# The order of loads, fills and sums set by kind of unit, large or small, in a shifted depthwise convolution

## The reference

```
def _L0_conv_ref(x, offset):          # 48 offsets, a multiple of 16 px plus a small draw
    off_px = offset * 64.0
    off_int = round(off_px)           # whole shift; sub = the rest
    shifted = x moved by off_int (dx, dy) per channel, zero outside
    kern = exp(-(kx*kx + ky*ky) / (2*0.5*0.5)); kern /= kern.sum()   # 3 x 3, from sub
    return depthwise_conv(shifted, kern, padding='SAME')

def _gn(v, G=32, eps=1e-5):
    g = v.reshape(B, G, C // G, H, W)
    return (g - mean(g)) / sqrt(var(g) + eps)

x = x + _L0_conv_ref(_gn(x), offset)
```

## Time and profile before

| what | value |
|---|---|
| median of 3 runs | 1114.45 us (1113.13 to 1116.01) |
| the profiled execution's own time | 1114.61 us |
| its span | 1112.8 us |
| mean granted TensorE clock | 0.872 |
| VectorE busy | 835.0 us, 75% |
| TensorE busy | 833.4 us, 75% |
| ScalarE busy | 661.0 us, 59% |
| moved by DMA | 403.07 MB, 362 GB/s over the span |

### The profile page before, as it was taken

How to read it: one execution, slowest core, us unless ns; L and a number is a source line. 1 busy time by engine, 2 the same in 40 slices (tenths; PEclk the granted TensorE clock), 3 DMA queues, 4 the chain that set the end, 5 groups by cost and what they waited for, 6 DMA issues and landing times. The chain is left out here.

```text
span 1112.8 us, 9630 instructions
## 1 busy us (share of the span) xinstructions
PE 833.4 (75%) x2176; PEld 399.4 (36%) x2176; DVE 835.0 (75%) x565; ACT 661.0 (59%) x547; POOL 170.7 (15%) x204
## 2 busy tenths in 40 slices
PE   6976986678688698759848887888888686888710
PEld 2432433234343244324324443343444343443310
DVE  8187696976948768696784968787887858659685
ACT  0564546565477574766556666556566474666771
POOL 3103131012110303201211110111112101102010
PEclk9988898989799898888969899898999889788955
DMA  9737979898899797989799999999999897997936
GB/s 373 309 148 274 430 291 400 345 382 373 343 403 412 287 429 320 410 328 398 319 347 429 396 402 428 398 429 398 430 398 433 336 426 305 399 431 306 373 160 292
DMA packets 27818, 403.07 MB, mean 362 GB/s; under 512 B 3216, under 2 KB 3216, under 8 KB 3216
## 3 DMA queue, kind: packets, MB, share of 16 engines
q1 hardware_dynamic: 27792, 402.71, 88.6%
HBM read 201.38 MB, written 201.33 MB: 362 GB/s over the span
## 5 line engine op out<-in xcount | busy, mean ns | idle before, releaser
L243 PE MATMUL sum_ps<-xs,bands 128*128 128x512 f32 x1024 | 505.4, 651 | 23.9 <-DMA xs<-x_dram 23.9
L346 ACT ACTIVATE unused<-xs,small 128x4096 bf16 (+1 forms) x96 | 356.1, 3709 | 20.7 <-ACT small L339 7.7
L499 DVE SCALAR_TENSOR_TENSOR smooth<-frame,xs 128x1700 f32 (+5 forms) x96 | 163.6, 1704 | 220.7 <-ACT frame L320 141.6
L243 PEld LDWEIGHTS sum_ps<-xs,bands 128*128 128x128 f32 x1024 | 209.1, 210 | 270.9 <-issue 267.5
L243 PE MATMUL sum_ps<-xs,halves 128*128 128x512 f32 x512 | 246.3, 637 | 74.2 <-DMA xs<-x_dram 74.2
L313 ACT ACTIVATE frame<-xs,small (+1 forms) x96 | 223.4, 2327 | 130.7 <-DVE smooth L502 128.2
L209 POOL TENSOR_TENSOR small<-small 128x3 f32<-128x3 f32 x32 | 60.9, 1902 | 900.3 <-ACT small L352 900.3
L506 DVE SCALAR_TENSOR_TENSOR xs<-smooth,small,xs 128x1700 f32 (+5 forms) x96 | 163.6, 1704 | 36.5 <-POOL small L221 34.0
L243 PEld LDWEIGHTS sum_ps<-xs,halves 128*128 128x128 f32 x512 | 102.3, 204 | 216.8 <-issue 122.8
L502 DVE SCALAR_TENSOR_TENSOR smooth<-frame,xs,smooth 128x1700 f32<-128x1700 f32 (+5 forms) x96 | 163.5, 1704 | 3.4
L509 DVE SCALAR_TENSOR_TENSOR xs<-smooth,small,xs 128x594 f32 (+9 forms) x96 | 159.8, 1665 | 3.4
(11 more groups left out here) (81 smaller groups left out, 279.0 us busy)
## 6 DMA issues: line engine op xcount, KB each, us to landing
xs<-x_dram SPq DMA_DIRECT2D x96, 2048.0 KB, 14.7
out_dram<-xs SPq DMA_DIRECT2D x96, 2048.0 KB, 11.8
smooth<-offset_dram SPq DMA_DIRECT2D x1, 48.0 KB, 4.0
```

The costliest lines, as they stand in the source:

```text
L243: last = nc.tensor.matmul(sum_ps[:, :], (FIRST, SAME, SECOND)[i], slot_px(n, c * BANK, (c + 1) * BANK), start=(i == 0 and c == 0), stop=(i ...
L346: nc.scalar.activation(unused[:, :], xs[:, bass.ds(n % SLOTS * PIX, PIX)], ACT.Square, bias=neg_mean[:, i:i + 1], accum_out=squares[:, i:i ...
L499: V.scalar_tensor_tensor(sm, frame_window(-1), side_w[:, bass.ds(n, 1), 0], frame_window(0), ALU.mult, ALU.add).wait_op(frame_ready, done_ ...
```

## The change

Three orders are changed, and nothing else.

- SyncE: of the six loads of a pair, those of tiles 6k+10 and 6k+14 move up by one store, ahead of the stores of tiles 6k+2 and 6k+6. The other four stay.
- TensorE: for u even, one tile of sums of u+1 comes before the variances of u and two behind it; for u odd it stays two and one.
- ScalarE: the units with u even use `large_unit`, where variances comes first and sum_means, means and the first square of u+1 come behind the fill of tile 1. The units with u odd use `small_unit`, which is the order before, but with the second square ahead of the fill of tile 2. The loop runs over pairs of units.

```diff
             for n in range(TILES):
                 store(n)
-                if 1 <= n <= TILES - SLOTS:
-                    load(n - 1 + SLOTS)
+                for i in AGAIN[n % len(AGAIN)]:
+                    m = n - n % len(AGAIN) + i + SLOTS
+                    if m < TILES:
+                        load(m)
...
             for u in range(UNITS):
-
+                ahead = 1 if u % 2 == 0 else 2
                 if u + 1 < UNITS:
-                    sums(u + 1, range(UT - 1))
+                    sums(u + 1, range(ahead))
                 variances(u)
                 if u + 1 < UNITS:
-                    sums(u + 1, range(UT - 1, UT))
+                    sums(u + 1, range(ahead, UT))
                     means(u + 1)
...
-            def unit_of(u, ahead=True):
-
+            def large_unit(u):
+
+                variances(u)
+                fill_frame(u, 0)
+                next_fill(u, 0)
+                fill_frame(u, 1)
+                next_fill(u, 1)
+                sum_means(u + 1)
+                means(u + 1)
+                square(u + 1, 0)
+                fill_frame(u, 2)
+                next_fill(u, 2)
+                means_to_fill(u + 1)
+                square(u + 1, 1)
+                square(u + 1, 2)
+
+            def small_unit(u, ahead=True):
                 fill_frame(u, 0)
                 next_fill(u, 0)
                 variances(u)
...
                 if ahead:
                     means(u + 1)
                     square(u + 1, 0)
+                    square(u + 1, 1)
                 fill_frame(u, 2)
                 if ahead:
                     next_fill(u, 2)
                     means_to_fill(u + 1)
-                    square(u + 1, 1)
                     square(u + 1, 2)
...
-            unit_of(0)
+            large_unit(0)
             act.addr_align(256, max_nops=0)
-            with act.Fori(1, UNITS - 1) as u:
-                unit_of(u)
-            unit_of(UNITS - 1, ahead=False)
+            with act.Fori(0, UNITS // 2 - 1) as pair:
+                small_unit(act.snap(2 * pair + 1))
+                large_unit(act.snap(2 * pair + 2))
+            small_unit(UNITS - 1, ahead=False)
```

More of the change, by code:

```diff
@@ L180, in _ @@
                 load(n)
+            AGAIN = [(), (0, 1), (), (2,), (3,), (4, 5)]
             for n in range(TILES):
                 store(n)
-                if 1 <= n <= TILES - SLOTS:
-                    load(n - 1 + SLOTS)
+                for i in AGAIN[n % len(AGAIN)]:
+                    m = n - n % len(AGAIN) + i + SLOTS
+                    if m < TILES:
+                        load(m)
             for s in range(SLOTS):
```

## The result

| kernel | median us (lowest to highest) | ratio to before, 95% interval |
|---|---|---|
| before | 1113.89 (1113.13 to 1116.01) | |
| after | 1124.53 (1123.15 to 1126.43) | 1.0094 [1.0073, 1.0114] |

The change costs 10.6 us, 0.94%. The forecast was 6.4 us slower, 1121.0; the sign and the range hold, and the forecast's own narrow range (1117.5 to 1127) holds it too.

A forecast was written before the change was run, and what follows sets the result against it. A chain through engines waiting in a ring sets the time, transfers close behind. Terms -2.8 (pairs 0, 1), -0.9 (4, 5), +1.8 (3200 pairs), +3.6 (8 to 11), +4.7 (14, 15) give +6.4: 1121.0 us, range 1105 to 1130.

The forecast's parts named there:

- The branch of two tiles: Two tiles of sums behind a large unit's variances take 16.6 us, making the third tile's fill late in some pairs.
- T: Time when TensorE has done a large unit's variances; the next was forecast at T+61.4, against 60.5 a pair before.
- The warm third tile: Sums of the next large unit's third tile, after a 1 to 2 us TensorE pause: 7.1 us in place of 9.53.
- pairs 8 to 11: Pairs with windows like pair 10, where the two-tile branch binds: +0.9 us each, +3.6 in all.
- pairs 14 and 15: First tiles of 900 and 1700 elements, where VectorE needs less time and the branch bites more: +4.7 us together.
- The six pairs of 3200 elements: Pairs 2, 3, 6, 7, 12, 13: VectorE's 18 us first tile covers the branch; net +1.8 us in all.
- Variances ahead of the fill: Large unit's first fill comes 1.7 us later, VectorE's 1.52 us wait for GpSimd goes; net +0.2 to +0.3 a pair.
- the fill ahead of sum_means: Fill of tile 6k+1 no longer waits for TensorE's sums; gain kept in pairs 0 and 1, -0.8 and -2.0 us.
- the other reading in the forecast: GpSimd's small instructions could stick beside VectorE's previous tile through shared SBUF interfaces, leaving up to 1.5 us of the wait.
- Pairs 0 and 1: VectorE leads by more than the branch needs, so they keep the gain of the earlier second fill: -2.8 us.
- The two loads: Loads issued up to 13 us earlier; no load ends last in the chain as read, so taken as 0.

The follow-up runs named there:

- e1: The changed kernel with TensorE's part undone, two tiles of sums ahead of the variances for every unit: 1116.71 us, 1.0021 of before.
- e5: The changed kernel itself, measured once more: 1124.67 us, 1.0094 of before.
- e3: The changed kernel with SyncE's part undone, store and load in turn: 1121.82 us, 1.0059 of before.
- e4: ScalarE's part of the change alone, with TensorE's and SyncE's orders as before: 1136.50 us, 1.0194 of before.
- e6: The changed kernel with large units' variances put back behind the fill of their first tile: 1124.07 us, 1.0088 of before.
- e8: The kernel before with second squares ahead of third fills, large units' sum_means behind the second fill, and the change's load order: 1095.48 us, 0.9841 of before.
- e9: The changed kernel with the register loads for the fills of tiles 1 and 2 moved behind the next square: 1096.23 us, 0.9830 of before.
- e11: The changed kernel with spare matmuls nobody reads, run while TensorE waits for ScalarE's squares: 1116.51 us, 1.0039 of before.
- e12: The best kernel (two squares ahead, register loads later) plus three spare matmul pairs before each unit's last square: 1091.72 us, 0.9805 of before.

## Why the prediction was right, and where its sizes were off

*The branch of two tiles* was read rightly, in time and in place. T+15.8 for the two tiles (mean over all large units 16.2, range 15.5 to 17.0, forecast 16.6), the third fill straight behind the square, 61.2 to the next T. `e1` takes the branch away and 8 of the 10.6 us with it: 10 us go in the six pairs where the forecast had it binding, and 3 are lost at the start.

*The warm third tile* was wrong. The forecast let TensorE's short pause ahead of this tile pass for none and took 7.1; it was 8.81 in pair 10, and 9.06 in the mean of fifteen, as before (9.00). Pair 10 shows that the pause there was short indeed: from 741 to 757 us TensorE was busy for 15.7 of 16 us at a granted clock of 1.00, then it did the small matmuls of the variances with 0.82 us of idle time among them, and the tile started at the upper level. A microsecond into the tile the granted clock was at 0.50, and it stayed there until about 762.5, with TensorE busy throughout. So the pause right in front of a tile does not tell whether it will be slow, and the forecast had told it by that. In pairs 8 to 11 this was offset by a first tile of 8.9 instead of 9.5 and by shorter steps to the fills: T+61.2 where T+61.4 was forecast, and +2.3 instead of +3.6 in the four. That the next T came so close is in part luck. In pairs 14 and 15 the third tile reached VectorE as forecast: F, the end of the large unit's last square, is 989.3 and 1053.9 (the fills below less the step of 1.97 that pair 12 has from square to fill, 846.05 to 848.02), and VectorE starts at F+26.5 and F+26.6, where F+27.0 was forecast and F+25.8 and F+24.05 stood before. ScalarE's fills and VectorE's instructions of after:

```profile
991.24 2.99 ACT L321 ACTIVATE frame<-xs,small  x1 [0.51 <-issue]
...
1055.87 2.99 ACT L321 ACTIVATE frame<-xs,small  x1 [0.51 <-issue]
```

```profile
1015.74 2.82 DVE L523 SCALAR_TENSOR_TENSOR smooth<-frame,xs 128x2500 f32 x1 [3.40 <-ACT frame L328]
...
1080.47 2.82 DVE L523 SCALAR_TENSOR_TENSOR smooth<-frame,xs 128x2500 f32 x1 [3.49 <-ACT frame L328]
```

*The six pairs of 3200 elements* are the mis-sized term: +0.3 each was forecast, +6.7 in all was measured, nearly the whole of what the forecast lacks. I had looked at them only up to VectorE's first tile, which covers the branch, and not at the small unit behind it. Pair 12 shows what is there. ScalarE and TensorE before:

```profile
883.60 8.59 PE L243 MATMUL sum_ps<-xs,bands 128*128 128x512 f32 x16
...
895.87 0.17 ACT L335 ACTIVATE small<-mean_ps 128x3 f32<-128x3 f32 x1 [0.25 <-issue]
...
903.76 0.20 ACT L339 ACTIVATE small<-small 128x3 f32<-128x3 f32 x1 [0.26 <-issue]
```

And after:

```profile
887.00 9.71 PE L249 MATMUL sum_ps<-xs,bands 128*128 128x512 f32 x16
...
901.03 0.17 ACT L343 ACTIVATE small<-mean_ps 128x3 f32<-128x3 f32 x1 [0.88 <-issue]
...
913.35 0.20 ACT L347 ACTIVATE small<-small 128x3 f32<-128x3 f32 x1 [0.71 <-issue]
```

The pair is 2.7 us longer, from VectorE's start on its first tile to the next such start. The tile of sums behind the small unit's variances is 1.1 us longer (9.71 for 8.59), and the two places behind a register load are 0.63 and 0.45 us longer. What is left, 0.5, is the step of variances and fill, for which 0.3 had been put.

Over all six pairs the share of the tile is small, and the register loads have the most of what was missed. The places behind a register load in the small unit are 3.6 us longer in sum (9.9 us for 6.2), the tile 0.8 and the step 2.9 (0.48 in each, 1.8 forecast): 7.3, where 6.7 was measured. In the trace of `e5` they are 4.0, -0.6 and 2.9, for 5.8 measured. The forecast had no term for these places at all, though rows of that kind stood in the trace of before. I can't say why pair 12's tile is colder after than before, as TensorE's pause ahead of it is shorter (8.4 us, from 878.6, against 10.8); nor why the register load takes longer. That it depends on the traffic of the moved loads would fit the difference between after and `e3`, where the two "issue" rows are 11.8 and 9.6 us instead of 16.0 and 12.3, and the six pairs have 5.9 us instead of 9.9. But the profiled execution of `e3` is the lowest of its seven, and in `e4`, with the old order of loads too, the six pairs have 9.1. The cause stays open.

*Variances ahead of the fill* and *the fill ahead of sum_means* came as forecast. The step takes 1.97 us in pair 12 (1.7 forecast), GpSimd's wait went in all sixteen large units, so that nothing of it stayed as the other reading in the forecast had it, and `e6` shows that the two cancel. Pairs 0 and 1 kept 1.6 of the 2.8.

*The two loads* were taken as 0. They cost 0 to 4 us (`e3`), and in `e8` no gain either. The reason given, that no load ends the chain, fits the one wait for a load that is left in after, at the start (10.8 us). It does not hold for the ScalarE part alone (`e4`), where the same two loads are worth 19 us: a load that is off the chain in one order of instructions stands on it in another.

## What to carry to other kernels

Where the trace shows a ring of engines that wait for each other, follow every branch through the whole ring, for each kind of stage; the term that was wrong here was the one for which a long instruction at the start seemed to cover all. A wait of a few tenths with no semaphore behind it is not noise if it recurs on an engine of the ring: count it over the kernel before anything else, on every engine (VectorE's row of this kind is untested here). Put work that is ready to run (here a second square, and the load of a register) in front of an instruction that waits, and not behind it.

## What the runs showed of the hardware

A load of a register from SBUF on ScalarE's queue is not free, though it doesn't count as busy. Its durations in after (least, median, most in ns) are:

```profile
L302 ACTq TENSOR_LOAD <-fills x96: 273/288/1340, 28.3 to 1100.0; - x96
```

The next instruction did not overlap the one before the load, as it does by 0.17 us without it, and started 0.24 to 1.2 us behind its end, by the load's own length; with the load behind a square of 3.71 us these gaps are gone (`e9`, 28 us). What makes one load four times as long as another is open. The Trainium skill (DMA: Bandwidth & Descriptors, Latency and other measured facts) states a floor of about 600 ns for such a load. Here half of them took under 0.3 us, and the longest 1.3.

A tile of sums took 7.0 us at a granted clock of 1.00 and up to 10.2 behind the variances. Spare matmuls brought the one tile behind a small unit's variances to 7.0 in all fifteen places (`e11`); but where TensorE was late already they stood in the way, and three pairs of them cost 12 us in the kernel in which it waits for transfers (`e12`).
